# First loads, 5x5 weight chores and the exchange of the fourth image's input statistics: a rearranged start of a two-convolution kernel

## The chip, the cores and the metric

The kernel runs on one core of one Trainium2 chip. The metric is the device time of one execution in microseconds (us), lower is better.

## What is computed

Sixteen images of 32 channels and 128x128 pixels go through two residual blocks, each a group normalization and a convolution:

```python
def _gn(v, G=16, eps=1e-05):            # 16 groups of 2 channels, per image
    ...
    return ((g - m) / jnp.sqrt(s + eps)).reshape(v.shape)
...
x = x + _L0_conv_ref(_gn(x), L0_conv_weight, L0_conv_threshold)   # 3x3, weights masked by a threshold
x = x + _L1_conv_ref(_gn(x), L1_conv_kernel, L1_conv_bias)        # 5x5, plus bias
```

The mask of the 3x3 weights depends on the sums of their absolute values over the output channels and on the scalar threshold, so no 3x3 weight can be used before all the weights and the threshold are on the chip.

## The kernel before

**Halves and steps.** Each image is cut into an upper and a lower half, so there are 32 halves (`HALVES`). A half lies on 128 partitions as 4 bands of rows by 32 channels. TensorE works in steps: step s does the 3x3 convolution of half s and the 5x5 convolution of half s - 3 (`LAG` is 3). Steps 0 to 2 do the 3x3 alone (the lead), steps 3 to 31 do both, steps 32 to 34 the 5x5 alone. Every value and weight is split into a high and a low float16 (`hi`, `lo`), and three of the four products are taken. Within a step TensorE does the 3x3 pairs (144 matmuls, `pairs3_high`, `pairs3_low`), then the high 5x5 pairs (320 matmuls, `pairs5_high`), the 3x3 singles, the 5x5 singles (their end signals `a5_whole`) and the low 5x5 pairs (their end signals `b5_whole`). The loop body is the same code in all steps; step 3 is its first pass. I call the start of `pairs5_high` in a step its 5x5 start.

**Statistics.** A half is normalized with the statistics of its whole image. VectorE takes them with `stats_in` (of `x_bands`, 4 instructions of 0.66 us for a half) and `stats_out` (of `mid`, the first block's result). The statistics of a group lie on several partitions and are combined in one of two ways. For images 0 and 1's input and image 0's middle, TensorE mixes them (`set_apart`, `mix_members`, `combine`). For all others they are exchanged through DRAM: VectorE's `aggregate` signals `mv_ready`, ScalarE's queue writes `mv` to `mv_scratch` (`spread_stats`), waits until that has landed, and reads all of it back to every partition as `every_mv` (`gather_stats`); then VectorE's `group_stats`, ScalarE's root and VectorE's `scale_of` give mean and scale. In what follows x2 and x3 are the input statistics of the third and fourth image (halves 4, 5 and 6, 7), mid1 the middle statistics of the second. Before, x2, mid1 and x3 are three exchanges, told off after steps 2, 3 and 4; from then on one exchange every two steps carries a middle and an input image together.

**Orders.** Each engine runs its own list in the order in which it is written, and waits for semaphores in that order. On ScalarE, at step s: take the 5x5 result of half s - 4 out of PSUM (`take_conv5`, 4 instructions), give TensorE leave for the 5x5 start (`x5_hi_go`), gather the exchange of step s - 1, normalize and split the coming halves, and last `spread_stats(s)`, which waits for `mv_ready`. GpSimd adds the 5x5 result to `mid` (`add_out`, L369), and in the lead it issues the 16 transfers of half 1 (L363). SyncE's queue (SPq) carries nearly all transfers: `load_bands` (L261, 4 of 288 KB for a half), `load_own` (L250), `move_mid` (L269, 16 transfers inside the chip), `store_out` (L255). The weights of both convolutions, threshold, mixing matrix and bias are loaded once: the 3x3 weights, the threshold and the matrix by ScalarE's queue (ACTq), the 5x5 weights and the bias by SPq behind three halves' bands.

**Last steps.** From half `LATE` on, ScalarE takes out two of the four banks of a 5x5 result and VectorE the other two (`take_late`, L757); before it, ScalarE takes all four.

## Time and profile before

| what | value |
|---|---|
| median of 3 runs | 823.47 us (822.88 to 823.75) |
| profiled execution, its own time | 823.28 us |
| its span in the trace | 821.5 us |
| TensorE matmul busy | 756.0 us (92%) |
| VectorE busy | 608.8 us (74%) |
| ScalarE busy | 333.9 us (41%) |
| GpSimd busy | 265.3 us (32%) |
| mean granted TensorE clock | 0.98 |

The span is what the trace covers; 1.8 us of the execution lie around it. Busy shares are means over the whole span, while the steps at the start and at the end have other limits than those between.

### The profile page before, as it was taken

Reading aid. Unit: us, or ns where it says so; the run is one execution under the profiler, and the core shown is the slowest. Engines: PE = TensorE matmul, PEld = TensorE weight load, DVE = VectorE, ACT = ScalarE, POOL = GpSimd, SP = SyncE. Lnnn points to the kernel's source line nnn. Section 1 sums busy time; section 2 is a strip of 40 time slices with the busy share of each in tenths; the row PEclk is TensorE's granted clock in tenths of the full one; section 3 lists DMA queues with packets and bytes.
Section 4 is the critical chain, followed back from the end, with each engine's and each line's share of the span. In section 5 each row is a group of like instructions: output and inputs, shape, how many; then the busy total and the mean of one; then the engine's idle time right before and its main releaser. Section 6 shows DMA issues by size and latency. Waiting matters only on the chain.

```text
span 821.5 us, 67804 instructions
## 1 busy us (share of the span) xinstructions
PE 756.0 (92%) x32292; PEld 528.7 (64%) x32292; DVE 608.8 (74%) x970; ACT 333.9 (41%) x289; POOL 265.3 (32%) x161
## 2 busy tenths in 40 slices
PE   0585898899999999999999999999999999998996
PEld 0252484568767667767766766776776676676664
DVE  2888757797878969787879878787878786663341
ACT  0252314344443636344443536353443436362420
POOL 1021034044434332233434343222434343322360
PEclk9997898999999999999999999999999999999998
DMA  9879399989997989899897979898997956673424
GB/s 203 158 143 224 75 217 227 230 205 220 195 222 171 220 195 221 196 218 212 202 217 168 219 183 227 196 225 198 215 219 181 220 116 161 137 167 86 99 51 102
DMA packets 234400, 150.76 MB, mean 184 GB/s; under 512 B 18752, under 2 KB 227712, under 8 KB 230272
## 3 DMA queue, kind: packets, MB, share of 16 engines
q1 hardware_dynamic: 227200, 143.93, 80.8%
q10 hardware_dynamic: 6464, 5.24, 2.7%
q0 software_dynamic: 704, 1.25, 0.6%
q8 instruction: 10, 0.16, 0.1%
q14 instruction: 22, 0.18, 0.1%
HBM read 75.86 MB, written 33.59 MB: 133 GB/s over the span
## 4 chain that ended last, share of the span: by engine, by line
PE 82%; DVE 8%; DMA 4%; issue 2%; DVEq 1%; ACT 1%; ACTq 1%
PE psum L868 63%; PE psum L886 20%; DMA every_mv<-mv_scratch 2%; DVE bn_in L615 2%; DMA thr<-L_conv_threshold_dram 1%; DVE x_lo L719 1%; DVE bn_out L747 1%; DMA mv_scratch<-mv 1%; DVE mid L739 1%; DVEq L742 1%; ACT conv_out L468 0%; ACTq L506 0%; ACTq L486 0%; DVE x_bands L691 0%; ACT x_hi L399 0%
## 5 line engine op out<-in xcount | busy, mean ns | idle before, releaser
L369 POOL TENSOR_TENSOR mid<-mid,conv_out 128x512 f32<-128x512 f32 x120 | 246.0, 2082 | 484.0 <-ACT conv_out L468 484.0
L868 PE MATMUL psum<-x_hi,s_hi 32*64 32x512 f16 x6656 | 201.3, 384 | 18.2 <-ACTq L506 6.2
L868 PE MATMUL psum<-x_lo,s_hi 32*64 32x512 f16 x6656 | 200.1, 383 | 5.9 <-DVE x_lo L719 5.9
L868 PE MATMUL psum<-x_hi,s_lo 32*64 32x512 f16 x6656 | 199.7, 381 | 0.0
L868 PEld LDWEIGHTS psum<-x_hi,s_hi 32*64 32x64 f16 x6656 | 122.0, 105 | 85.9 <-issue 11.2
L868 PEld LDWEIGHTS psum<-x_hi,s_lo 32*64 32x64 f16 x6656 | 133.6, 105 | 53.6 <-issue 4.3
L868 PEld LDWEIGHTS psum<-x_lo,s_hi 32*64 32x64 f16 x6656 | 108.9, 104 | 83.8 <-issue 11.6
L739 DVE SCALAR_TENSOR_TENSOR mid<-psum,unscale,x_own 128x1024 f32<-128x1024 f32 x64 | 79.1, 1278 | 90.5 <-PE psum L886 90.4
L468 ACT ACTIVATE conv_out<-psum,bias,unscale 128x512 f32<-128x512 f32 x120 | 83.7, 777 | 69.7 <-PE psum L868 60.7
L392 ACT ACTIVATE x_hi<-x_bands 128x2304 f16<-128x2304 f32 x31 | 65.6, 2117 | 106.2 <-PE psum L886 106.2
L727 DVE TENSOR_TENSOR x_lo<-mid_bands,x_hi 128x2560 f16<-128x2560 f32 x32 | 93.8, 2932 | 6.9 <-PE psum L868 6.8
L431 ACT ACTIVATE x_hi<-mid_bands 128x2560 f16<-128x2560 f32 x31 | 72.5, 2339 | 50.8 <-PE psum L886 48.8
L385 ACT ACTIVATE root<-gvar 128x1 f32<-128x1 f32 x32 | 6.5, 203 | 207.7 <-DVE gvar L668 175.2
L438 ACT ACTIVATE mid_bands<-mid_bands,nbias,gscale 128x2560 f32<-128x2560 f32 x31 | 78.2, 2524 | 16.0 <-DVE nbias L682 13.6
L747 DVE BATCH_NORM_STATS2 bn_out<-mid 128x6 f32<-128x512 f32 x128 | 79.1, 680 | 4.1
L719 DVE TENSOR_TENSOR x_lo<-x_bands,x_hi 128x2304 f16<-128x2304 f32 x32 | 80.7, 2522 | 0.6 <-ACT x_hi L392 0.2
L615 DVE BATCH_NORM_STATS2 bn_in<-x_bands 128x6 f32<-128x512 f32 x128 | 76.7, 663 | 2.6 <-DMA x_bands<-x_dram 2.6
L886 PE MATMUL psum<-x_hi,s_hi 32*32 32x512 f16 x4096 | 74.3, 378 | 1.8 <-issue 1.7
L886 PE MATMUL psum<-x_hi,s_lo 32*32 32x512 f16 x4096 | 73.4, 376 | 0.0
L691 DVE TENSOR_SCALAR x_bands<-x_bands,gmean,gscale 128x2304 f32<-128x2304 f32 x29 | 67.8, 2339 | 0.5 <-ACT x_hi L403 0.4
L886 PE MATMUL psum<-x_lo,s_hi 32*32 32x512 f16 x4096 | 66.2, 377 | 1.4 <-issue 1.4
L886 PEld LDWEIGHTS psum<-x_hi,s_hi 32*32 32x32 f16 x4096 | 53.6, 88 | 19.7 <-issue 15.7
(91 smaller groups left out, 338.3 us busy)
## 6 DMA issues: line engine op xcount, KB each, us to landing
x_own<-x_dram SPq DMA_DIRECT2D x128, 256.0 KB, 5.0
mid_bands<-mid SPq DMA_DIRECT2D x372, 80.0 KB, 3.4
out_dram<-mid SPq DMA_DIRECT2D x116, 256.0 KB, 5.3
x_bands<-x_dram SPq DMA_DIRECT2D x96, 288.0 KB, 6.1
x_bands<-x_dram SPq DMA_DIRECT2D x32, 272.0 KB, 6.9
mid_bands<-mid SPq DMA_DIRECT2D x124, 64.0 KB, 2.9
every_mv<-mv_scratch ACTq DMA_DIRECT2D x17, 256.0 KB, 4.1
out_dram<-mid SPq DMA_DIRECT2D x20, 128.0 KB, 2.4
```

The lines of the kernel that those rows point to most:

```text
L369: nc.gpsimd.tensor_tensor(m, m, conv_out[:, b, :], ALU.add).then_inc(out_added, 1)
L431: nc.scalar.activation(x5_hi[:, :, 2:2 + W], mid_bands[:, k % MB_SLOTS, :, :], ACT.Copy).then_inc(hi5_done, 1)
L438: nc.scalar.activation(v, v, ACT.Identity, bias=nbias[:, at], scale=gscale[:, at]).then_inc(act_scaled, 1)
L468: nc.scalar.activation(conv_out[:, b, :], psum[:, X5_BANK + b, :], ACT.Identity, bias=bias[:, 0:1], scale=unscale[:, 1:2]).then_inc(conv5_ ...
L615: nc.vector.bn_stats(bn_in[:, h // 2 % 2, h % 2, b, :], rows.rearrange("p a w -> p (a w)")).then_inc(bn_x, 1)
L691: nc.vector.tensor_scalar(v, v, gmean[:, 0:1], gscale[:, 0:1], ALU.subtract, ALU.mult).then_inc(scaled, 1)
L719: nc.vector.tensor_tensor(x3_lo[:, :, 2:2 + W], x_bands[:, h % XB_SLOTS, :, :], x3_hi[:, :, 2:2 + W], ALU.subtract).then_inc(x3_lo_go, 1)
L727: nc.vector.tensor_tensor(x5_lo[:, :, 2:2 + W], mid_bands[:, k % MB_SLOTS, :, :], x5_hi[:, :, 2:2 + W], ALU.subtract).then_inc(x5_lo_go, 1)
L739: nc.vector.scalar_tensor_tensor(mid[:, h % MID_SLOTS, at, :], psum[:, X3_BANK + at.start:X3_BANK + at.stop, :], unscale[:, 0:1], x_own[:, ...
L747: nc.vector.bn_stats(bn_out[:, h % 2, b, :], mid[:, h % MID_SLOTS, b, :]).then_inc(bn_mid, 1)
L868: ins = nc.tensor.matmul(psum[2 * C * J:2 * C * (J + 1), bank + i, :].rearrange("p (a w) -> p a w", a=A), w[quad(i), at:at + 2, :].rearran ...
L886: ins = nc.tensor.matmul(psum[quad(j), bank + i, :].rearrange("p (a w) -> p a w", a=A), w[quad(i), at, :], src[quad(i), j + dy:j + dy + A ...
```

## The change

The change does six things. (1) Two of the four copies of the 3x3 weights are issued by SPq ahead of all bands, the other two by ACTq ahead of the threshold. (2) The 5x5 weights move ahead of the third half's bands, and the bias moves to ACTq with a semaphore of its own. (3) The largest absolute 5x5 weight is looked for while TensorE mixes image 0's statistics; the 5x5 weights are scaled by GpSimd, rounded to float16 by ScalarE after its `high3(3)`, and the low part is made by GpSimd. (4) Bands of halves 6 and 7 are issued right behind `move_mid(2)`, no longer behind the wait for `a5_whole`. (5) x3 and mid1 share one exchange after step 3, so there is none after step 4. (6) `LATE` is one half earlier.

```diff
-        mv_dram = nc.dram_tensor("mv_scratch", (N + 1, P, 2, 2), F32, kind="Internal").ap()
+        mv_dram = nc.dram_tensor("mv_scratch", (N, P, 2, 2), F32, kind="Internal").ap()
...
         def exchanged(s):
 
-            if s in (2, LAG + 1):
-                return [("x", 2 if s == 2 else LAG)]
+            if s == 2:
+                return [("x", 2)]
             if not (LAG <= s < HALVES and s % 2):
                 return []
-            return [("mid", s // 2)] + ([("x", (s + 3) // 2)] if LAG < s and (s + 3) // 2 < N else [])
+            return [("mid", s // 2)] + ([("x", (s + 3) // 2)] if (s + 3) // 2 < N else [])
...
-        LATE = HALVES - LAG
+        LATE = HALVES - LAG - 1
...
+            for q in range(Q // 2):
+                sp.dma_start(w3[quad(q), :, :], w3_dram.rearrange("i a b o -> i (a b) o")).then_inc(w3_loaded, 16)
             load_bands(0)
             load_bands(1)
-            load_bands(2)
             for q in range(Q):
                 sp.dma_start(w5[quad(q), :, :], w5_dram.rearrange("i a b o -> i (a b) o")).then_inc(w_loaded, 16)
-                sp.dma_start(bias[quad(q), :], bias_dram.rearrange("(o a) -> o a", a=1)).then_inc(w_loaded, 16)
+            load_bands(2)
...
             load_bands(5)
             move_mid(2)
+            load_bands(6)
+            load_bands(7)
             sp.wait_ge(a5_whole, 1)
             load_own(LAG + 1)
             move_edges(1, 1, 0)
-            load_bands(6)
-            load_bands(7)
...
+            pool.wait_ge(w5_bounded, 1)
+            nc.gpsimd.tensor_scalar(w5[:, :, :], w5[:, :, :], wfac[:, 1:2], None, ALU.mult).then_inc(w5_scaled, 1)
+            pool.wait_ge(w5_hi_made, 1)
+            nc.gpsimd.tensor_tensor(s5_lo[:, :, :], w5[:, :, :], s5_hi[:, :, :], ALU.subtract).then_inc(w5_split, 1)
...
             def high_w5():
 
-                act.wait_ge(w5_bounded, 1)
-                nc.scalar.activation(s5_hi[:, :, :], w5[:, :, :], ACT.Identity,
-                                     bias=zeros[:, 0:1], scale=wfac[:, 1:2]).then_inc(w5_hi_made, 1)
+                act.wait_ge(w5_scaled, 1)
+                nc.scalar.activation(s5_hi[:, :, :], w5[:, :, :], ACT.Copy).then_inc(w5_hi_made, 1)
...
-            for q in range(Q):
+            for q in range(Q // 2, Q):
                 act.dma_start(w3[quad(q), :, :], w3_dram.rearrange("i a b o -> i (a b) o")).then_inc(w3_loaded, 16)
             act.dma_start(thr[:, :], thr_dram.rearrange("(a o) -> a o", a=1).to_broadcast([P, 1])).then_inc(w3_loaded, 16)
             act.dma_start(mix_in[:, :], mix_dram).then_inc(mix_loaded, 16)
+            for q in range(Q):
+                act.dma_start(bias[quad(q), :], bias_dram.rearrange("(o a) -> o a", a=1)).then_inc(bias_loaded, 16)
...
-                    high_w5()
                 elif s == 2:
                     high3(3)
+                    high_w5()
                     take_root(("mid", 0))
...
             set_apart("x", 0)
+            dve.wait_ge(w_loaded, 16 * Q)
+            largest(w5, 1)
             dve.drain().then_inc(bank3_go, 1)
...
-            dve.wait_ge(w_loaded, 16 * 2 * Q)
-            largest(w5, 1)
             power_of_two(1)
...
-            dve.wait_ge(w5_hi_made, 1)
-            nc.vector.scalar_tensor_tensor(s5_lo[:, :, :], w5[:, :, :], wfac[:, 1:2], s5_hi[:, :, :],
-                                           ALU.mult, ALU.subtract).then_inc(w5_split, 1)
             normalize5_first()
...
             stats_out(LAG)
-            aggregate("mid", LAG // 2, mv_ready)
             low3(LAG + 1)
+            stats_in(2 * LAG, range(BANKS))
+            stats_in(2 * LAG + 1, range(BANKS))
+            aggregate("mid", LAG // 2)
+            aggregate("x", LAG, mv_ready)
...
-                if s == LAG + 1:
-                    for h in (2 * LAG, 2 * LAG + 1):
-                        stats_in(h, range(BANKS))
-                    aggregate("x", LAG, mv_ready)
-                elif exchanged(s):
+                if exchanged(s):
```

How the instructions move on three engines follows, with the line numbers of each version. First SyncE's queue at the first pass of the loop, before: the first rows are the end of `load_bands(5)` and `move_mid(2)`.

```order
L261 DMA x_bands<-x_dram 32x2304 x3
L261 DMA x_bands<-x_dram 32x2176
L269 DMA mid_bands<-mid 32x5x128 x2
L269 DMA mid_bands<-mid 32x4x128 x2
L269 DMA mid_bands<-mid 32x5x128 x8
L269 DMA mid_bands<-mid 32x4x128 x2
L269 DMA mid_bands<-mid 32x5x128 x2
L250 DMA x_own<-x_dram 32x16x128 x4
L280 DMA mid_bands<-mid 32x128 x2
L261 DMA x_bands<-x_dram 32x2176
L261 DMA x_bands<-x_dram 32x2304 x6
L261 DMA x_bands<-x_dram 32x2176
```

The same place of SyncE's queue with the change:

```order
L263 DMA x_bands<-x_dram 32x2304 x3
L263 DMA x_bands<-x_dram 32x2176
L271 DMA mid_bands<-mid 32x5x128 x2
L271 DMA mid_bands<-mid 32x4x128 x2
L271 DMA mid_bands<-mid 32x5x128 x8
L271 DMA mid_bands<-mid 32x4x128 x2
L271 DMA mid_bands<-mid 32x5x128 x2
L263 DMA x_bands<-x_dram 32x2176
L263 DMA x_bands<-x_dram 32x2304 x6
L263 DMA x_bands<-x_dram 32x2176
L252 DMA x_own<-x_dram 32x16x128 x4
```

The eight transfers of bands 6 and 7 (2.3 MB) now stand ahead of the `x_own` loads, which keep the wait for `a5_whole`.

Second, VectorE from the normalization of half 4 on, at the end of step 3, before:

```order
L691 TENSOR_SCALAR x_bands<-x_bands,gmean,gscale 128x2304
L696 MEMSET x_bands 32x128
L739 SCALAR_TENSOR_TENSOR mid<-psum,unscale,x_own 128x1024 x2
L747 BN_STATS bn_out<-mid 128x6 x4
L625 BN_AGGR mv<-bn_out 128x2
L719 TENSOR_TENSOR x_lo<-x_bands,x_hi 128x18x128
L727 TENSOR_TENSOR x_lo<-mid_bands,x_hi 128x20x128
```

With the change:

```order
L702 TENSOR_SCALAR x_bands<-x_bands,gmean,gscale 128x2304
L707 MEMSET x_bands 32x128
L750 SCALAR_TENSOR_TENSOR mid<-psum,unscale,x_own 128x1024 x2
L758 BN_STATS bn_out<-mid 128x6 x4
L730 TENSOR_TENSOR x_lo<-x_bands,x_hi 128x18x128
L626 BN_STATS bn_in<-x_bands 128x6 x8
L636 BN_AGGR mv<-bn_out 128x2
L636 BN_AGGR mv<-bn_in 128x2
L738 TENSOR_TENSOR x_lo<-mid_bands,x_hi 128x20x128
```

The signal for the exchange, which stood at the first BN_AGGR, now stands at the last one, behind the low part of half 4 and the eight statistics instructions of halves 6 and 7.

Third, ScalarE at the same place, from the write and read of the x2 exchange on. Before:

```order
L475 DMA mv_scratch<-mv 128x4
L481 DMA every_mv<-mv_scratch 128x512
L385 ACTIVATE root<-gvar 128x1
L438 ACTIVATE mid_bands<-mid_bands,nbias,gscale 128x2560
L460 ACTIVATE mid_bands<-zeros 32x256
L392 ACTIVATE x_hi<-x_bands 128x18x128
L431 ACTIVATE x_hi<-mid_bands 128x20x128
L475 DMA mv_scratch<-mv 128x4
L468 ACTIVATE conv_out<-psum,bias,unscale 128x512 x4
L481 DMA every_mv<-mv_scratch 128x512
L385 ACTIVATE root<-gvar 128x1
```

With the change:

```order
L484 DMA mv_scratch<-mv 128x4
L490 DMA every_mv<-mv_scratch 128x512
L393 ACTIVATE root<-gvar 128x1
L445 ACTIVATE mid_bands<-mid_bands,nbias,gscale 128x2560
L467 ACTIVATE mid_bands<-zeros 32x256
L400 ACTIVATE x_hi<-x_bands 128x18x128
L438 ACTIVATE x_hi<-mid_bands 128x20x128
L484 DMA mv_scratch<-mv 128x4
L477 ACTIVATE conv_out<-psum,bias,unscale 128x512 x4
L490 DMA every_mv<-mv_scratch 128x512
L393 ACTIVATE root<-gvar 128x1 x2
```

The rows are in the same order, with a second root behind the last read. The second `mv_scratch` write, behind which `take_conv5(0)` and TensorE's leave for step 4's 5x5 start stand, now waits for the later signal of VectorE.

## Rows read from the trace of the kernel before

**Rows 1.** Busy by stretch: us, PE, PEld, DVE, ACT, POOL, PEclk, DMA share, GB/s.

```profile
109.42:137.43 28.01, 24.37 (x1021) 17.99 (x1012) 19.68 (x33) 10.36 (x9) 9.00 (x6) 0.93 1.14 228
...
137.43:167.22 29.79, 26.22 (x1016) 15.64 (x1008) 19.43 (x34) 10.29 (x9) 7.26 (x5) 0.89 1.03 208
...
167.22:190.02 22.80, 22.80 (x1020) 16.93 (x1012) 21.99 (x39) 11.24 (x11) 10.05 (x4) 1.00 0.98 218
```

**Rows 2.** Chain of waits in order of time (start us, us, what), first load.

```profile
3.83 11.01 DMA thr<-L_conv_threshold_dram
```

**Rows 3.** DMA issues (KB, us to landing), made at 2.1, 2.1 and 5.0.

```profile
w<-L_conv_weight_dram ACTq DMA_DIRECT2D x1, 36.0 KB, 7.8
...
x_bands<-x_dram SPq DMA_DIRECT2D x1, 288.0 KB, 8.2
...
x_bands<-x_dram SPq DMA_DIRECT2D x1, 288.0 KB, 9.5
```

**Rows 4.** Timeline (start us, us, engine, operation), VectorE before step 3.

```profile
28.85 0.17 DVE L643 COPY members<-psum 128x16 f32<-128x16 f32 x1 [0.77 <-PE psum L930]
...
57.67 0.98 DVE L569 TENSOR_REDUCE bound<-w 128x1 f32<-128x800 f32 x1
```

**Rows 5.** Timeline, page part 5 and timeline again: GpSimd.

```profile
55.71 9.21 POOL L363 DMA_DIRECT2D mid_bands<-mid  x16 [50.73 <-DVE mid L739]
...
L369 POOL TENSOR_TENSOR mid<-mid,conv_out 128x512 f32<-128x512 f32 x120 | 246.0, 2082 | 484.0 <-ACT conv_out L468 484.0
...
782.64 6.41 POOL L377 TENSOR_SCALAR mid<-mid,bias 128x2048 f32<-128x2048 f32 x1
```

**Rows 6.** Timeline: ScalarE root of image 0, SyncE move_mid(2).

```profile
67.46 0.20 ACT L385 ACTIVATE root<-gvar 128x1 f32<-128x1 f32 x1 [3.95 <-DVE gvar L653]
...
72.10 11.58 SPq L269 DMA_DIRECT2D mid_bands<-mid  x16
```

**Rows 7.** Timeline: third image's input statistics and their exchange.

```profile
82.14 2.48 DVE L615 BATCH_NORM_STATS2 bn_in<-x_bands 128x6 f32<-128x512 f32 x4 [2.62 <-DMA x_bands<-x_dram]
...
85.05 0.34 ACTq L475 DMA_DIRECT2D mv_scratch<-mv  x1
...
88.31 0.33 ACTq L481 DMA_DIRECT2D every_mv<-mv_scratch  x1
...
91.74 0.41 DVE L660 SCALAR_TENSOR_TENSOR product<-every_mv,mix_in 128x128 f32<-128x128 f32 x1 [4.39 <-DMA every_mv<-mv_scratch]
```

**Rows 8.** Chain of waits: later exchange transfers.

```profile
108.76 10.11 DMA every_mv<-mv_scratch
...
132.43 7.69 DMA mv_scratch<-mv
...
140.14 8.00 DMA every_mv<-mv_scratch
```

**Rows 9.** Timeline of TensorE in its first whole step.

```profile
81.56 3.20 PE L868 MATMUL psum<-x_hi,s_hi 32*64 32x512 f16 x51 [5.24 <-issue]
...
97.96 0.39 PE L886 MATMUL psum<-x_hi,s_hi 32*32 32x512 f16 x4 [1.74 <-issue]
```

**Rows 10.** Busy time by stretch, columns as in rows 1.

```profile
88.00:92.00 4.00, 3.93 (x207) 2.47 (x192) 0.26 (x1) 0.00 (x0) 0.00 (x0) 1.00 0.24 74
```

**Rows 11.** Timeline: VectorE and ScalarE, steps 4 and 5.

```profile
101.79 2.50 DVE L719 TENSOR_TENSOR x_lo<-x_bands,x_hi 128x2304 f16<-128x2304 f32 x1
...
127.16 4.83 DVE L615 BATCH_NORM_STATS2 bn_in<-x_bands 128x6 f32<-128x512 f32 x8
...
132.86 2.79 ACT L468 ACTIVATE conv_out<-psum,bias,unscale 128x512 f32<-128x512 f32 x4 [3.02 <-DVE mv L625]
...
122.27 2.52 ACT L438 ACTIVATE mid_bands<-mid_bands,nbias,gscale 128x2560 f32<-128x2560 f32 x1 [1.19 <-DVE nbias L682]
```

**Rows 12.** Timeline of TensorE at the last 5x5 starts.

```profile
759.61 4.61 PE L868 MATMUL psum<-x_hi,s_hi 32*64 32x512 f16 x160 [2.96 <-ACTq L506]
...
778.25 4.61 PE L868 MATMUL psum<-x_hi,s_hi 32*64 32x512 f16 x160 [1.61 <-ACTq L506]
```

More of the change, by code:

```diff
@@ L125, in two_blocks @@
         w5_bounded = sem("w5_bounded")
+        bias_loaded = sem("bias_loaded")
+        w5_scaled = sem("w5_scaled")
         w5_hi_made = sem("w5_hi_made")
@@ L373, in _ @@
                     add_out(k, b)
-                if k == LATE:
+                if k == LATE + 1:
+                    pool.wait_ge(bias_loaded, 16 * Q)
                     pool.wait_ge(norm2, HALVES)
@@ L463, in take_conv5 @@
             def take_conv5(k, b):
+                if k == 0 and b == 0:
+                    act.wait_ge(bias_loaded, 16 * Q)
                 act.wait_ge(b5_whole, k + 1)
@@ L500, in _ @@
                         take_conv5(k, b)
-                if HALVES < s <= LAST + LAG:
-                    act.wait_ge(late_out, s - HALVES)
+                if LATE + LAG < s <= LAST + LAG:
+                    act.wait_ge(late_out, s - LATE - LAG)
                 if s == LAG:
@@ L752, in take_late @@
                 if k == LATE:
+                    dve.wait_ge(bias_loaded, 16 * Q)
                     dve.wait_ge(out_added, BANKS * LATE)
@@ L810, in _ @@
             stats_out(LAG)
-            aggregate("mid", LAG // 2, mv_ready)
             low3(LAG + 1)
+            stats_in(2 * LAG, range(BANKS))
+            stats_in(2 * LAG + 1, range(BANKS))
+            aggregate("mid", LAG // 2)
+            aggregate("x", LAG, mv_ready)
             for s in range(LAG + 1, STEPS):
                 gathered = exchanged(s - 1)
-                if s > HALVES:
+                if s > LATE + LAG:
                     take_late(s - 1 - LAG)
                 low5(s - LAG)
-                if s > HALVES:
+                if s > LATE + LAG:
                     add_late(s - 1 - LAG)
-                just_now = ("x", (s + 1) // 2) in gathered
-                if has3(s + 1) and not just_now:
+                if has3(s + 1):
                     normalize3(s + 1)
@@ L829, in _ @@
                     scale_of(stat)
-                if just_now:
-                    normalize3(s + 1)
                 if s % 2:
```

## The prediction

> **What bounds the kernel now.** I read the chain of waits first. From step 6 to the tail it is TensorE's matmuls alone. I then cut the span at TensorE's 5x5 starts and read busy time by stretch. In the third row of [rows 1] one whole step takes 22.80 us, all of it busy, at full clock; the chain shows this step repeated until the tail, so nothing in the change can shorten it. The two steps before it take 28.01 and 29.79 us, 12.2 us more than two full ones, with idle time and a granted clock of 0.93 and 0.89. Ahead of them lie 109.4 us of start. So there are three places where time can come from: the start, these two steps, and the stops of 2.96 and 1.61 us in the tail [rows 12].
>
> What fills the start is told by the chain: first the threshold, which lands 11.01 us after its issue, at 14.8 us [rows 2], then VectorE nearly without a gap until step 3, then the x2 exchange. What fills the two steps are the mid1 and x3 exchanges: 10.11 us for one read, 7.69 and 8.00 us for the next write and read [rows 8], while the x2 exchange took only 3.3 us and 3.4 us [rows 7]. The difference is the traffic beside it: at 88 to 92 us the DMA share is 0.24, in the two steps it is 1.14 and 1.03 [rows 1, 10].
>
> **Weights first by two queues.** The last 3x3 weights, issued at 2.1 us, land at 9.9 us, the fourth band issued at the same time at 10.3, the eighth band at 5.0 + 9.5 = 14.5 us [rows 3], the threshold at 14.8 [rows 2]. Counted in partition rows, ACTq had then moved 4 x 32 of weights and 128 of threshold, SPq 8 x 32 of bands: 256 each, and 128 each at 9.9 and 10.3. The queues take turns row by row, whatever a row holds. With the change 64 + 128 = 192 ACTq rows bring the threshold; SPq's first 192 rows are 64 of weights and 128 of bands, which is the content that had landed at 10.3 us. The bands are issued 0.9 us later, so between 10.3 and 11.2; I take 10.8, **4.0 us earlier**. Bounds: 2.2 us if only its earlier issue counted (two issues fewer ahead), 4.5 at best.
> In the Trainium skill, "DMA: Bandwidth & Descriptors", section "Issuing engines are not separate DMA queues", using several issuing engines only saves issue time. By that rule this term would be 2.2 us. It is a rival below.
>
> **The 5x5 chores.** VectorE's search for the largest weight (0.98 us) moves into a wait of 0.77 us [rows 4]: it adds 0.3 us there and takes 1.0 us away before step 3. The 5x5 weights have landed by then: they are 0.4 MB behind two halves, whose last band came at 14.5, and VectorE gets there at about 24. So VectorE runs 3.7 us ahead of before until 54, then 4.7. On the other side GpSimd is free only when its 16 transfers are issued, 55.71 + 9.21 - 3.7 = 61.2 us. Its scaling costs 6.41 x 800/2048 = 2.5 us, its subtraction 2.08 x 800/512 = 3.3 us [rows 5]. ScalarE rounds from 63.8 to 64.9 and only then takes image 0's root, at 64.9 where before it was 67.46 [rows 6]: of the 4.7 us only 2.6 remain. The low weights are ready at 68.2, before ScalarE has the first 5x5 input (69.2). This delay is covered: x2's statistics wait 2.62 us for half 5's band [rows 7], and that band depends on SPq alone, which moves by 3.7. If GpSimd is slower by more than some 1.5 us, each further one counts.
>
> **The x2 exchange in traffic.** It starts 3.7 us earlier, at 85.05 - 3.7 = 81.3. But `move_mid(2)`, issued from 72.10 for 11.58 us [rows 6], ends at 80.0 now, and behind it come bands 6 and 7 at once, no longer after the first pass. Those are 2.3 MB, at about 218 GB/s, between the 208 and 228 of [rows 1], 10.6 us: DMA is full until about 93. By turns of rows the 128 small rows of the write take as long as in [rows 8], 7.7; I take 7.4, until 88.7. The read (128 rows) is in traffic for 4 of its us and then free: 7.0, between the free 3.4 and the full 10.1. x2 lands at **95.7**, where a free exchange would have landed at 88.0.
>
> **The joint exchange.** From x2's landing to the end of the low part of half 4 VectorE needed 101.79 + 2.50 - 91.74 = 12.55 us [rows 7, 11]. Now come the eight statistics, 4.83 us, and one more aggregate, 0.3: `mv_ready` at 95.7 + 17.7 = 113.4 instead of 101.9. What is queued behind it on ScalarE is `take_conv5(0)` and the leave for the 5x5 start. That engine already shows this wait, 3.02 us before 132.86 [rows 11]. Add 0.4 and 2.8 for four takings: TensorE's 5x5 start of step 4 comes at **116.7, 7.3 us later** than 109.42. TensorE itself would be there at 109.42 - 2.6 plus the slower code loads below, 2 to 6: at 109 to 113.
> After that x3 is known, and the 12.2 us of the two steps fall away, except for a lower clock after the stop of step 4. In the two steps busy time was 1.6 and 3.4 us over a full step's 22.80 [rows 1]; I take 2.1, since the step after the stop has no second one. Is the joint read in time for step 5? It is issued at 116.9 and takes 8.0. Behind the read that landed at 108.76 + 10.11 = 118.9, ScalarE began to normalize at 122.27 [rows 8, 11], 3.4 us for one statistic; for two I take 6.8, so 131.7. Then it normalizes for 2.5 us and splits half 5 in about as long: ready at 136.7. The 144 pair matmuls of a 3x3 take 144 x 4.61/160 = 4.1 us [rows 12], so step 5 starts at 116.7 + 22.8 - 4.1 + 2.1 = 137.5. In time by 0.8 us.
> Sum of this part: +7.3 - 12.2 + 2.1 = **-2.8 us**. The weights' 4.0 us are already in it, since they set the 81.3.
>
> **The tail.** Step 32's stop of 2.96 us becomes one of 1.61, since ScalarE takes two banks and VectorE, idle there, the others [rows 12]: **-1.35 us**. The bias, now on ACTq, is needed a hundred us later: nothing.
>
> **Sum.** 823.28 (the profiled execution's own time) - 2.8 - 1.35 = 819.1. The runs' median is 0.2 higher, so I give **819.2 us**. A measurement here tells 0.2% (1.6 us) from no change.
>
> **Code loading.** TensorE stands still for 5.24 us at 76.3 to 81.56 and for 1.74 us before 97.96 with nothing to wait for but its own code [rows 9], which this pass meets for the first time; the long stop lies in full DMA traffic, the short one in none. Bands 6 and 7 now bring traffic to two or three more such loads. I expect 2 to 6 us more, hidden in the wait for 116.7.
> The skill's "Runtime: NRT & Kernel Launch", section "Instruction fetch mechanics", calls such crossings mostly hidden. The 5.24 us disagree; by the rule the pass would end earlier and the sum would be the same.
>
> **The rivals.**
> *Bands 6 and 7 don't hurt x2* (its write and read keep 3.3 and 3.4 us): `mv_ready` at 88.0 + 17.7 = 105.7, 5x5 start at 109.0, no stop behind it: -0.4 - 12.2 - 1.35, so 809.3. For it: the traffic is of known length, and the write's rows are tiny. Against: [rows 8]. Chance 0.15.
> *The queues' rule* holds: everything in the start is 1.8 us later, 821.0. Chance 0.08.
> *Code loading takes over*: three further stops at 5.2 instead of 1.4 to 1.7 are +11 us on the first pass, and the 5x5 start comes at 109.42 - 2.6 + 11 = 117.8 plus a clock not yet recovered, some 1.6: +2.7, 821.8. Chance 0.17.
> *Slower*: exchanges in traffic take their worst row. x2's read takes 10.1: 5x5 start at 119.8, +3.1. The joint read takes 10.1 too, half 5 is ready at 120 + 10.1 + 6.8 + 5.0 = 141.9, 1.3 after the step's start at 140.6, and the stop lowers the clock once more, 2.1: 823.3 - 4.15 + 3.1 + 1.3 + 2.1 = 825.6. It decides once both exchanges together are more than 4 us over my figures. For it: 10.11 us is a row of this trace; against: the joint read meets no backlog of bands. Chance 0.15.
> *The forecast*, 816 to 822: chance 0.45.
>
> **Numbers.** Range 810 to 825: it reaches to the first rival and leaves out most of the last and half of the first. Faster by over 0.2%: nearly all of the forecast, the first rival, the rule and part of code loading, 0.70. Within 0.2%: 0.15. Slower: 0.15.
>
> **What would show it.** In the trace after: first mask instruction of VectorE near 10.9 us; image 0's root near 65; x2's write at 81 and its read back near 96; DMA full from 82 to 93; `mv_ready` near 113; a stop of TensorE before step 4's 5x5 start near 116.7, none before step 6; one stop of 1.6 us where 2.96 was. Wrong would make it: an x2 landing outside 93 to 99, a first pass ending after 112, or a second stop before step 5.

## The result: 814.4 us, 1.1% faster than before

| | changed | before, beside it |
|---|---|---|
| median | 814.38 us | 823.61 us |
| runs | 4 (813.69 to 816.45) | 4 (822.88 to 825.56) |
| ratio | 0.9887 (0.9871 to 0.9902) | |
| profiled execution, its span | 814.51 us, 812.7 us | 823.28 us, 821.5 us |
| mean granted clock | 0.985 | 0.98 |

The kernel became 9.2 us faster; 4.3 us were forecast. The time lies inside the range and has the sign of the forecast, but the gain is twice as large, so one of the steps must be wrong. (Two later timings of the same change, further down, give gains of 7.3 and 8.1 us.) Each step is now compared, in the order of the program. In the changed kernel most line numbers are higher than before, by 2 to 11: L873 and L891 are the matmuls, L484 and L490 the exchange's write and read, L517 the leave for the 5x5 start.

**The start.** DMA issues of the changed kernel (KB, us from issue to landing), made at 2.1 and 1.66 us:

```profile
x_bands<-x_dram SPq DMA_DIRECT2D x1, 288.0 KB, 5.1
...
thr<-L_conv_threshold_dram ACTq DMA_DIRECT2D x1, 0.5 KB, 6.2
```

Timeline of VectorE in the changed kernel (start us, us, engine, operation, idle before and who ended it):

```profile
7.96 0.46 DVE L603 TENSOR_REDUCE score<-w 128x9 f32<-128x288 f32 x1 [6.15 <-DMA thr<-L_conv_threshold_dram]
...
21.01 0.98 DVE L580 TENSOR_REDUCE bound<-w 128x1 f32<-128x800 f32 x1
22.13 0.17 DVE L654 COPY members<-psum 128x16 f32<-128x16 f32 x1
```

The threshold lands at 7.86 us; [rows 2] had 14.84. So the first mask instruction starts at 7.96, not near 10.9, and the copy of the mixed sums at 22.13 where [rows 4] has 28.85: 6.7 us earlier. The search for the largest weight (21.01) fills the wait before that copy, as expected. Between the two VectorE takes the eight statistics of the first two halves without waiting for their bands. In other executions it does wait for the second half's bands, as shown below, so these are the next floor of the start.

**The 5x5 chores.** Timelines of GpSimd, ScalarE and VectorE in the changed kernel:

```profile
58.37 2.29 POOL L368 TENSOR_SCALAR w<-w,wfac 128x800 f32<-128x800 f32 x1
61.64 1.71 POOL L370 TENSOR_TENSOR s_lo<-w,s_hi 128x800 f16<-128x800 f32 x1 [0.98 <-ACT s_hi L431]
...
60.69 0.87 ACT L431 ACTIVATE s_hi<-w 128x800 f16<-128x800 f32 x1 [4.20 <-POOL w L368]
61.47 0.19 ACT L393 ACTIVATE root<-gvar 128x1 f32<-128x1 f32 x1
...
75.07 2.47 DVE L626 BATCH_NORM_STATS2 bn_in<-x_bands 128x6 f32<-128x512 f32 x4 [0.48 <-DMA x_bands<-x_dram]
```

ScalarE's rounding waits for GpSimd and image 0's root follows at 61.47, 6.0 us earlier than in [rows 6]. GpSimd's subtraction takes 1.71 us, not 3.3. Half 5's statistics still wait for their band, now 0.48 us instead of the 2.62 of [rows 7]: the chores are covered, though only just.

**The x2 exchange.** Timeline of SyncE's queue, ScalarE's queue and VectorE, then busy time by stretch (us, PE, PEld, DVE, ACT, POOL, PEclk, DMA share, GB/s), changed kernel:

```profile
76.78 5.14 SPq L263 DMA_DIRECT2D x_bands<-x_dram  x8
77.98 0.35 ACTq L484 DMA_DIRECT2D mv_scratch<-mv  x1
85.77 0.35 ACTq L490 DMA_DIRECT2D every_mv<-mv_scratch  x1
91.90 0.39 DVE L671 SCALAR_TENSOR_TENSOR product<-every_mv,mix_in 128x128 f32<-128x128 f32 x1 [11.62 <-DMA every_mv<-mv_scratch]
...
84.00:88.00 4.00, 0.74 (x44) 0.30 (x24) 0.00 (x0) 0.00 (x0) 0.00 (x0) 1.00 1.04 230
88.00:92.00 4.00, 1.71 (x73) 1.27 (x80) 0.10 (x1) 0.00 (x0) 0.00 (x0) 0.64 0.48 114
```

Bands 6 and 7 are issued at 76.78, the write behind them takes 7.8 us until 85.77 and the read 6.1 us until 91.90. Before it was 3.3 and 3.4 [rows 7]. Although the exchange starts 7.1 us earlier than before, x2 lands 0.2 us later. The DMA share beside it is 1.04 from 84 to 88 us and 0.48 from 88 to 92, when the bands are in; before, with the exchange in about the same place, [rows 10] had 0.24.

**From x2 to step 6.** Timelines of ScalarE's queue, ScalarE, TensorE and VectorE at step 4's 5x5 start, then the stretches between 5x5 starts, changed kernel:

```profile
109.65 0.33 ACTq L484 DMA_DIRECT2D mv_scratch<-mv  x1
110.08 2.78 ACT L477 ACTIVATE conv_out<-psum,bias,unscale 128x512 f32<-128x512 f32 x4 [8.09 <-DVE mv L636]
112.95 6.26 PE L873 MATMUL psum<-x_hi,s_hi 32*64 32x512 f16 x160 [3.46 <-ACTq L517]
112.97 0.33 ACTq L490 DMA_DIRECT2D every_mv<-mv_scratch  x1
117.11 1.31 DVE L671 SCALAR_TENSOR_TENSOR product<-every_mv,mix_in 128x128 f32<-128x128 f32 x1 [2.23 <-DMA every_mv<-mv_scratch]
...
112.95:116.00 3.05, 3.05 (x64) 1.56 (x72) 1.84 (x2) 0.00 (x0) 3.05 (x3) 0.51 0.79 172
...
112.95:137.44 24.49, 24.49 (x1009) 15.96 (x1016) 18.95 (x38) 11.23 (x11) 8.10 (x5) 0.93 1.07 229
137.44:160.20 22.76, 22.76 (x1016) 17.31 (x1008) 17.70 (x21) 9.44 (x8) 8.02 (x5) 1.00 0.93 205
```

ScalarE's taking of the 5x5 result waits 8.09 us for the joint `mv_ready`, and TensorE stops for 3.46 us before its 5x5 start at 112.95, 3.5 us later than the 109.42 of [rows 1]. The 160 matmuls behind the stop take 6.26 us instead of 4.6, since the granted clock is 0.51, about the lower level of 1.2 GHz, up to 116. The joint read is issued 3.3 us after the write, but the write is not what it waits for: it lands 1.8 us after its issue, and the read stands behind ScalarE's four takings. The read takes 4.1 us. After that there is no stop: 24.5 and 22.8 us stand where [rows 1] has 28.01 and 29.79. Step 6's 5x5 start is at 160.20, before it was at 167.22: **7.0 us** are won by here.

**Code loading.** Timeline of TensorE in the first pass, changed kernel:

```profile
76.18 1.73 PE L873 MATMUL psum<-x_hi,s_hi 32*64 32x512 f16 x51 [2.31 <-issue]
81.30 2.61 PE L873 MATMUL psum<-x_hi,s_lo 32*64 32x512 f16 x83 [1.41 <-issue]
90.29 0.61 PE L891 MATMUL psum<-x_hi,s_hi 32*32 32x512 f16 x4 [5.55 <-issue]
```

Three stops with no releaser, and two more of 1.09 and 1.01 us follow at 98 and 102: 11.4 us in sum. Before it was 8.4: the 5.24 and 1.74 of [rows 9] and one of 1.44 us between them, which [rows 9] leaves out. That these are code loads is seen in the DMA queues. Between 84.7 and 90.3 us the changed kernel has

```profile
q8 instruction: 1, 0.02, 1.5%
```

that is, one transfer of 16 KB on the instruction queue, and one such transfer lies in each of these stops or ends within 0.4 us ahead of it, in both kernels; from step 4's 5x5 start to step 6's this queue moves nothing. The pass ends before 109.5 all the same, ahead of the leave at 112.95.

**The tail.** Timeline of TensorE at the 5x5 starts of steps 32 and 33, changed kernel:

```profile
750.79 4.60 PE L873 MATMUL psum<-x_hi,s_hi 32*64 32x512 f16 x160 [1.61 <-ACTq L517]
769.43 4.60 PE L873 MATMUL psum<-x_hi,s_hi 32*64 32x512 f16 x160 [1.62 <-ACTq L517]
```

The stop of 2.96 us of [rows 12] is one of 1.61. From step 6's 5x5 start to the end it is 652.5 us, before 654.3: **1.8 us** are won here, 1.35 of them by this stop.

### The profile page after: what moved, and what is told of

Same layout as the page of the kernel before. It is cut to its first block, busy times and chain, and to the rows that moved or that the text cites. A ratio compares the mean times of both kernels' runs of the same rounds, so it can differ in the third digit from the quotient of the medians.

```text
span 812.7 us, 67805 instructions
## 1 busy us (share of the span) xinstructions
PE 751.7 (92%) x32292; PEld 503.0 (62%) x32292; DVE 615.3 (76%) x971; ACT 332.3 (41%) x287; POOL 264.6 (33%) x161
## 4 chain that ended last, share of the span: by engine, by line
PE 85%; DMA 5%; SPq 4%; DVE 3%; issue 1%; DVEq 0%; ACT 0%; ACTq 0%
PE psum L873 65%; PE psum L891 20%; DMA x_bands<-x_dram 3%; SPq L271 1%; DVE bn_in L626 1%; SPq L263 1%; SPq L252 1%; DMA mv_scratch<-mv 1%; DMA every_mv<-mv_scratch 1%; DVE x_lo L730 1%; ACT conv_out L477 0%; DVE x_bands L702 0%; SPq L278 0%; DVE mid L750 0%; DVEq L753 0%
## 5 line engine op out<-in xcount | busy, mean ns | idle before, releaser
L376 POOL TENSOR_TENSOR mid<-mid,conv_out 128x512 f32<-128x512 f32 x118 | 241.2, 2075 | 481.5 <-ACT conv_out L477 481.5
L873 PE MATMUL psum<-x_hi,s_hi 32*64 32x512 f16 x6656 | 199.6, 383 | 16.4 <-ACTq L517 8.3
L873 PE MATMUL psum<-x_lo,s_hi 32*64 32x512 f16 x6656 | 197.5, 380 | 6.3 <-DVE x_lo L730 5.3
L873 PE MATMUL psum<-x_hi,s_lo 32*64 32x512 f16 x6656 | 196.5, 377 | 1.4 <-issue 1.4
L873 PEld LDWEIGHTS psum<-x_hi,s_hi 32*64 32x64 f16 x6656 | 107.3, 105 | 98.5 <-ACTq L517 10.2
L873 PEld LDWEIGHTS psum<-x_hi,s_lo 32*64 32x64 f16 x6656 | 127.0, 104 | 58.9 <-issue 2.8
L873 PEld LDWEIGHTS psum<-x_lo,s_hi 32*64 32x64 f16 x6656 | 102.6, 104 | 87.2 <-issue 9.8
L891 PE MATMUL psum<-x_hi,s_hi 32*32 32x512 f16 x4096 | 74.7, 380 | 6.6 <-issue 6.6
L891 PE MATMUL psum<-x_hi,s_lo 32*32 32x512 f16 x4096 | 74.3, 380 | 0.0
L891 PEld LDWEIGHTS psum<-x_hi,s_hi 32*32 32x32 f16 x4096 | 54.3, 88 | 24.5 <-issue 20.6
L891 PE MATMUL psum<-x_lo,s_hi 32*32 32x512 f16 x4096 | 68.0, 384 | 0.1
```

The source lines that it names most:

```text
L376: nc.gpsimd.tensor_tensor(m, m, conv_out[:, b, :], ALU.add).then_inc(out_added, 1)
L873: ins = nc.tensor.matmul(psum[2 * C * J:2 * C * (J + 1), bank + i, :].rearrange("p (a w) -> p a w", a=A), w[quad(i), at:at + 2, :].rearran ...
L891: ins = nc.tensor.matmul(psum[quad(j), bank + i, :].rearrange("p (a w) -> p a w", a=A), w[quad(i), at, :], src[quad(i), j + dy:j + dy + A ...
```

## The experiments

"Its before" is the kernel before, timed on the same chip together with it. All kernels compute the whole reference. The theories: **T1**, the small transfers ahead give more than turns of rows allow, and this is most of the gain; **T2**, bands 6 and 7 beside the x2 exchange take back what the joint exchange gives; **T3**, the one half more for `take_late` gives 1.35 us.

| kernel | median us (its before) | ratio (interval) |
|---|---|---|
| weights part alone | 818.68 (825.24) | 0.9925 (0.9897 to 0.9952) |
| changed, weights part undone | 822.64 (825.24) | 0.9970 (0.9954 to 0.9985) |
| changed, weights behind the first half | 817.85 (825.24) | 0.9915 (0.9886 to 0.9944) |
| changed, exchanges apart, bands 6, 7 late | 816.39 (825.24) | 0.9898 (0.9867 to 0.9929) |
| changed, second time | 816.18 (823.50) | 0.9918 (0.9888 to 0.9947) |
| changed, bands 6, 7 behind x2 | 809.05 (823.50) | 0.9823 (0.9790 to 0.9856) |
| the same, chores as before | 807.57 (823.50) | 0.9799 (0.9765 to 0.9832) |
| changed, all weights by SPq | 816.06 (823.50) | 0.9899 (0.9867 to 0.9932) |
| changed, third time | 815.46 (823.57) | 0.9897 (0.9846 to 0.9947) |
| changed, `LATE` undone | 820.19 (823.57) | 0.9948 (0.9926 to 0.9970) |
| changed, chores undone | 816.49 (823.57) | 0.9898 (0.9848 to 0.9948) |
| bands 6, 7 behind x2, chores as before, bands 4, 5 early | 808.13 (823.57) | 0.9810 (0.9760 to 0.9860) |
| changed, `LATE` undone, second time | 819.45 (823.07) | 0.9954 (0.9938 to 0.9970) |
| before, second profile | 822.45 (823.07) | one run |
| bands 6, 7 behind x2, chores as before, all weights by SPq | 806.45 (823.07) | 0.9806 (0.9788 to 0.9823) |

**The weights part alone, and everything but it.** The first is the kernel before with this edit; the second is the changed kernel with it undone.

```diff
+            for q in range(Q // 2):
+                sp.dma_start(w3[quad(q), :, :], ...).then_inc(w3_loaded, 16)
             load_bands(0)
...
-            for q in range(Q):
+            for q in range(Q // 2, Q):
                 act.dma_start(w3[quad(q), :, :], ...).then_inc(w3_loaded, 16)
```

> The kernel before with one part of the change: two quarters of the 3x3 weights issued by SyncE's queue ahead of all bands, two by ScalarE's ahead of the threshold. Theory (the start alone gave most of the gain, about 7.0 us, and the tail 1.8; the joint exchange with early bands is worth about nothing): VectorE's first mask instruction near 8 us, x2's write near 78, x2 landed near 85, total about 7 us below before, 816.6 (815.8 to 817.8). Rival (the forecast's sum: the start gives less than 4 us by itself and the rest of the change the other 5): 819.5 to 820.5.

> The changed kernel with the weights' part undone: all four quarters by ScalarE's queue behind one another, bands first on SyncE's. Theory: VectorE's first mask instruction back near 14.9 us, everything up to step 6 some 6.5 to 7 us later than in the changed kernel, total 821.0 (820.3 to 821.8). Rival (the joint exchange and the early bands carry the gain): 816 to 818.

The weights part alone wins 6.6 us (by its interval 4.0 to 8.5), everything else together 2.6 (1.2 to 3.8); the sum is the 9.2 measured. Both times lie above the ranges expected, since the kernel before took 825.24 us on this chip; the distances to it are the expected ones. T1 holds for the size of the weights part by these times. The one profile of that kernel doesn't show it: it is of its slowest execution (821.79 us), in which the mask starts at 10.57 us, only 4.4 us earlier than before. In the first kernel the two later stops stay, as its timeline of TensorE shows:

```profile
131.92 2.79 PE L870 MATMUL psum<-x_lo,s_hi 32*64 32x512 f16 x48 [4.57 <-DVE x_lo L721]
...
161.65 0.65 PE L870 MATMUL psum<-x_lo,s_hi 32*64 32x512 f16 x16 [2.74 <-DVE x_lo L721]
```

In the second, VectorE starts the mask late, and x2's write and read (ScalarE's queue, then VectorE's first use) show that the exchange suffers without the weights part too:

```profile
14.53 0.45 DVE L601 TENSOR_REDUCE score<-w 128x9 f32<-128x288 f32 x1 [12.73 <-DMA thr<-L_conv_threshold_dram]
...
84.73 0.35 ACTq L482 DMA_DIRECT2D mv_scratch<-mv  x1
89.05 0.35 ACTq L488 DMA_DIRECT2D every_mv<-mv_scratch  x1
99.61 0.38 DVE L669 SCALAR_TENSOR_TENSOR product<-every_mv,mix_in 128x128 f32<-128x128 f32 x1 [12.58 <-DMA every_mv<-mv_scratch]
```

4.3 and 10.6 us: a sum of 14.9, against 13.9 in the changed kernel and 6.7 before.

**Where the weights stand.** Two edits of the changed kernel: SPq issues its two weight quarters behind `load_bands(0)`; or SPq issues all four ahead of the bands, and ACTq begins with the threshold.

```diff
-            for q in range(Q // 2): sp.dma_start(w3...)
             load_bands(0)
+            for q in range(Q // 2): sp.dma_start(w3...)
```
```diff
-            for q in range(Q // 2): sp.dma_start(w3...)
+            for q in range(Q): sp.dma_start(w3...)
...
-            for q in range(Q // 2, Q): act.dma_start(w3...)
```

> The changed kernel with SyncE's two weight quarters issued behind the four transfers of the first half's bands instead of ahead of them; ScalarE's queue is as changed. If the queues take turns row by row from the start, the last of weights and threshold lands at about 10.8 us, 3 us later than in the changed kernel, total 817.3. If what matters is only what stands ahead of the threshold on ScalarE's own queue, it lands near 8 and SyncE's quarters near 10, total 816.5. If the ahead-of-all-bands place matters because weights and threshold then move before the bands' backlog forms, threshold and weights land later than 11 us: 818 or more.

> The changed kernel with all four quarters of the 3x3 weights on SyncE's queue ahead of the bands and the threshold alone first on ScalarE's. If a place ahead of the bands' backlog is what counts, weights and threshold have all landed by 5 us, VectorE starts near 5 and then waits for the second half's band (which lands near 16 to 18): total 0 to 2 us below the changed kernel. If ScalarE's queue is slow whatever stands on it, no difference.

DMA issue of the threshold at 1.66 us and timeline of VectorE in the first kernel:

```profile
thr<-L_conv_threshold_dram ACTq DMA_DIRECT2D x1, 0.5 KB, 6.4
...
10.67 0.45 DVE L603 TENSOR_REDUCE score<-w 128x9 f32<-128x288 f32 x1 [8.87 <-DMA w<-L_conv_weight_dram]
```

Timeline of VectorE in the second:

```profile
5.60 0.45 DVE L601 TENSOR_REDUCE score<-w 128x9 f32<-128x288 f32 x1 [3.79 <-DMA w<-L_conv_weight_dram]
...
18.71 2.47 DVE L624 BATCH_NORM_STATS2 bn_in<-x_bands 128x6 f32<-128x512 f32 x4 [2.64 <-DMA x_bands<-x_dram]
23.01 0.17 DVE L652 COPY members<-psum 128x16 f32<-128x16 f32 x1
```

In the first kernel the bands start at 0.73 us as they did before, and still the threshold lands at 8.1. What VectorE waits for are SPq's two quarters, issued at 3.5 us and later. This run decides on the turns. By turns the threshold, at the end of ACTq's 192 rows, would be due with SPq's first 192 rows, the first half's four bands and the two quarters, near the 10.8 us of the expectation. These rows did come at 10.6. The threshold came at 8.1, when SPq had landed three bands, some 100 rows; the fourth landed at 9.5. That the mask starts near 10.8 here is therefore no support for the turns. The time of this kernel, 0.9915 of its before, can't be told from that of the changed kernel (0.9887, 0.9918 and 0.9897 in three timings): that the two quarters stand ahead of the bands, and not behind the first half's, is not shown to gain anything.

With all of the weights ahead the mask starts at 5.60, but VectorE then waits for bands, 2.64 us before the second half's statistics, and the copy comes at 23.01, no earlier than 22.13. The time stays that of the changed kernel.

**The changed kernel twice more**, to see how much of this varies.

> The changed kernel once more, on the chip of the next three, so that they can be read against it: 9 us below before, as measured first.

> The changed kernel once more on the chip of the next three, to read them against it: 7 to 9 us below before.

The change wins 7.3 and 8.1 us here, where the first timing gave 9.2. The mask starts at 7.64 and 6.91 us, the copy comes at 22.94 and 21.48. Over all eleven profiles with the weights ahead by two queues the mask starts between 5.75 and 10.57 us (in seven of them up to 8.3, in four from 9.9 on) and the copy comes between 21.5 and 24.7; with the old order the three profiles give 14.94 (behind the threshold of [rows 2]), 14.80 and 14.53. Where the mask starts before 8 us, the copy comes between 21.5 and 23.2 without following it, since VectorE then mostly waits for the second half's bands. The x2 write varies too. VectorE and ScalarE's queue in the second profile:

```profile
18.64 2.47 DVE L626 BATCH_NORM_STATS2 bn_in<-x_bands 128x6 f32<-128x512 f32 x4 [1.03 <-DMA x_bands<-x_dram]
...
78.99 0.35 ACTq L484 DMA_DIRECT2D mv_scratch<-mv  x1
90.09 0.35 ACTq L490 DMA_DIRECT2D every_mv<-mv_scratch  x1
```

**Exchanges apart.** The changed kernel with x3 and mid1 exchanged apart and bands 6 and 7 loaded behind the first pass, as before.

```diff
-            if s == 2:
-                return [("x", 2)]
+            if s in (2, LAG + 1):
+                return [("x", 2 if s == 2 else LAG)]
...
-            load_bands(6)
-            load_bands(7)
             sp.wait_ge(a5_whole, 1)
             load_own(LAG + 1)
             move_edges(1, 1, 0)
+            load_bands(6)
+            load_bands(7)
```

> The changed kernel with separate exchanges for mid1 and x3 and bands 6 and 7 behind the wait for a5_whole, as before; weights, chores and LATE as changed. Theory (joint exchange with early bands nets to zero: 5x5 start of step 4 ten us earlier, two slow steps of 12 us instead of one stop): 814.5 (813.5 to 815.7). Rival (the joint exchange was worth the forecast's 2.8 us or more): 817 to 819.

0.9898 against 0.9887, 0.9918 and 0.9897 of the changed kernel, on other chips: parts 4 and 5 of the change together show no gain. One or two microseconds either way could hide in the intervals. Without them x2's write and read take 3.0 and 4.0 us, and the stops of 3.43, 2.86 and 1.43 us in steps 5 and 6 are back.

**Bands 6 and 7 held until x2 has landed.** The changed kernel with one wait more.

```diff
             move_mid(2)
+            sp.wait_ge(mv_in, 16)
             load_bands(6)
             load_bands(7)
```

> The changed kernel, but SyncE issues bands 6 and 7 only when x2's read has landed (a wait on mv_in), so that exchange has the DMA to itself. Theory (the early bands take back what the joint exchange gives, by slowing x2's write and read): x2's write and read take 3.3 and 3.4 us again, x2 lands near 85 instead of 92, the 5x5 start of step 4 comes 1 to 6 us earlier (TensorE's code loads then meet the bands' traffic), total 2 to 4 us below the changed kernel. Rival (TensorE's first pass bounds that place, not x2): same as the changed kernel within 1 us.

Timeline of ScalarE's queue, VectorE, SyncE's queue, ScalarE and TensorE, and the stretch of the exchange:

```profile
78.48 0.35 ACTq L485 DMA_DIRECT2D mv_scratch<-mv  x1
81.62 0.35 ACTq L491 DMA_DIRECT2D every_mv<-mv_scratch  x1
85.06 0.48 DVE L672 SCALAR_TENSOR_TENSOR product<-every_mv,mix_in 128x128 f32<-128x128 f32 x1 [4.29 <-DMA every_mv<-mv_scratch]
85.05 4.78 SPq L263 DMA_DIRECT2D x_bands<-x_dram  x8
...
103.75 2.79 ACT L478 ACTIVATE conv_out<-psum,bias,unscale 128x512 f32<-128x512 f32 x4 [3.52 <-PE psum L874]
107.38 4.57 PE L874 MATMUL psum<-x_hi,s_hi 32*64 32x512 f16 x160
...
78.00:82.00 4.00, 4.00 (x128) 2.15 (x118) 2.74 (x6) 0.00 (x0) 0.00 (x0) 0.75 0.29 44
```

This is the cleanest of the tests: 7.1 us faster than the changed kernel on the same chip. Write and read are at 3.1 and 3.4 us, DMA at 0.29; `mv_ready` comes at 103.0, ScalarE takes the 5x5 result when TensorE has it, and TensorE reaches the 5x5 start at 107.38 without a stop; in the changed kernel's second profile, on the same chip, it was 114.56, 7.2 us later. T2 holds, and its price is larger than the 2 to 4 us I had expected of it. Beside the kernel with the exchanges apart (0.9898 of its before, here 0.9823, and the intervals don't meet) it shows too what the joint exchange is worth once x2's is left alone: some 6 us.

**The chores.** ScalarE rounds with the scale, in its old place (`high_w5` in step 1), and VectorE makes the low part as before; first in the kernel with the added wait, then in the changed kernel.

```diff
-            nc.gpsimd.tensor_scalar(w5[:, :, :], w5[:, :, :], wfac[:, 1:2], None, ALU.mult).then_inc(w5_scaled, 1)
...
-            nc.gpsimd.tensor_tensor(s5_lo[:, :, :], w5[:, :, :], s5_hi[:, :, :], ALU.subtract).then_inc(w5_split, 1)
...
+            nc.vector.scalar_tensor_tensor(s5_lo[:, :, :], w5[:, :, :], wfac[:, 1:2], s5_hi[:, :, :],
+                                           ALU.mult, ALU.subtract).then_inc(w5_split, 1)
```

> As the run with bands 6 and 7 behind x2's read, and in addition the 5x5 weights are scaled by ScalarE and split by VectorE as before (the search for the largest stays in its new place). If GpSimd's share of the chores delays TensorE's first whole step (x_lo of half 3 came 3.7 us late in the changed kernel) and that step now bounds, total a further 1 to 3 us lower. If not, no difference.

> The changed kernel with the 5x5 weights scaled by ScalarE and split by VectorE as before. In the changed kernel the delay by GpSimd is covered by the wait for half 5's band and later by x2's landing, so the root of image 0 comes 2 us earlier and x_lo of step 3 three us earlier, and the total stays (within 1 us of the changed kernel). If the delay were not covered, 2 to 3 us below it.

No difference outside the intervals: 807.57 beside 809.05, and 816.49 beside 815.46. VectorE arrives earlier at half 5's statistics and waits 3.53 and 3.67 us there for the band, instead of 0.5 to 1.0.

**Bands 4 and 5 early.** To the kernel with the added wait and the chores as before: is that band the next bound?

```diff
             load_own(1)
+            load_bands(4)
+            load_bands(5)
             sp.wait_ge(mid_made, PIECES)
...
-            load_bands(4)
...
-            load_bands(5)
```

> The version with bands 6 and 7 behind x2's read and the chores back, and in addition bands 4 and 5 issued in the first load, where DMA stood idle from 36 to 40 us, instead of behind the moves of half 0. VectorE's wait of 3.5 us for half 5's band goes, x2's write starts 3 us earlier; TensorE's code loads of the first pass meet less traffic. If x2 still bounds step 4's start: 2 to 3 us below that version (807.6), 804.5 to 805.5. If TensorE's first pass bounds it by now: 0 to 1.5 us below.

Timeline of ScalarE in this kernel:

```profile
68.71 2.52 ACT L418 ACTIVATE x_hi<-mid_bands,nbias,gscale 128x2560 f16<-128x2560 f32 x1 [8.45 <-DMA mid_bands<-mid]
```

The wait for the band is gone, but the copies inside the chip now land behind these bands: ScalarE waits 8.45 us for `mid_bands`, TensorE 6.28 us for ScalarE's leave at 71.77, and x2's write starts no earlier (81.95). One wait took the place of the other, and neither expected outcome came: 808.13 us beside 807.57 is no gain.

**`LATE` undone**, in the changed kernel, twice, and the kernel before once more.

```diff
-        LATE = HALVES - LAG - 1
+        LATE = HALVES - LAG
...
-                if k == LATE + 1:
+                if k == LATE:
```

> The changed kernel with LATE where it was. The stop before the 5x5 start of step 32 is 2.96 us again instead of 1.61; total 1.35 us above the changed kernel (0.8 to 2.2). Rival (the sharing by VectorE costs elsewhere what it saves): no difference.

> The changed kernel with LATE where it was, again, since it came out 4.7 us above the changed kernel where 1.35 was expected. If the excess is the start's variation (first mask instruction at 10.5 us in that profile) plus the stop of step 32 and the clock lost behind it, the profile shows the stop of 2.96 us each time, the next 5x5 start 18.6 or 20.3 us later, and a ratio to before of 0.990 to 0.996. If it was chance, the ratio is 0.991 or below.

> The kernel before, profiled a second time. If the landing of the threshold varies from execution to execution as it does with the weights first (VectorE's first mask instruction stood between 6.3 and 10.6 us in ten profiles), it should stand somewhere between 12 and 18 us here instead of 14.94; if it is fixed by what stands ahead in the queues, at 14.9 within 0.5. The last 5x5 starts after step 32's stop come 18.6 us apart if no clock is lost there, 20.3 if it is.

It costs 4.7 us on the same chip, where T3 says 1.35. Timeline of TensorE at the last 5x5 starts and the stretch behind the stop, the second of the two, then the kernel before profiled again:

```profile
753.33 7.48 PE L873 MATMUL psum<-x_hi,s_hi 32*64 32x512 f16 x160 [2.94 <-ACTq L517]
774.83 4.61 PE L873 MATMUL psum<-x_hi,s_hi 32*64 32x512 f16 x160 [1.60 <-ACTq L517]
...
753.33:756.00 2.67, 2.67 (x56) 1.26 (x64) 0.02 (x1) 0.00 (x0) 2.67 (x3) 0.50 0.68 186
756.00:759.00 3.00, 3.00 (x72) 1.35 (x64) 1.97 (x5) 0.00 (x0) 2.14 (x2) 0.50 0.66 146
```
```profile
758.78 4.60 PE L868 MATMUL psum<-x_hi,s_hi 32*64 32x512 f16 x160 [2.95 <-ACTq L506]
777.41 4.60 PE L868 MATMUL psum<-x_hi,s_hi 32*64 32x512 f16 x160 [1.61 <-ACTq L506]
...
758.78:762.00 3.22, 3.22 (x120) 1.90 (x128) 0.02 (x1) 0.00 (x0) 3.22 (x3) 1.00 0.71 193
```

The stops are equal, 2.94 and 2.95 us. But behind the first the granted clock is 0.50 (the 1.2 GHz level) for some 5.7 us, and the next 5x5 start comes 21.50 us later instead of 18.63, so 2.9 us are lost a second time. In the other profile with `LATE` undone it is 20.27 (1.6 lost), and so it is for the weights part alone (20.20), which has the old `LATE` too. Both profiles of the kernel before lose nothing.

**All together, and all weights by SPq**: the wait before bands 6 and 7, the chores as before, and the order of weights of the earlier test.

> The version with bands 6 and 7 behind x2's read and the chores back, with all 3x3 weights on SyncE's queue ahead of the bands and the threshold first on ScalarE's. VectorE starts near 5.6 us and is then held by the second half's bands, so image 0's mix is taken up at 23.0 us, 1.1 us before that version's profile (24.07): ratio to before 0.001 to 0.002 below its 0.980. If the start does not reach through to step 4 any more (TensorE's code loads bound it), no difference.

806.45 us (806.18 to 807.01), 16.6 us under its before. It has the lowest median of all, but the other kernels with the held bands lie within some 2.6 us of it and were timed on other chips, so only the wait is shown to matter. Its mask starts at 5.29 us, and from step 3 on TensorE's longest stops are two code loads, 5.05 and 6.12 us.

## Why the forecast was half of the gain

**The step that failed** is the one under "Weights first by two queues": "The queues take turns row by row, whatever a row holds." From it came a threshold that lets VectorE start at 10.8, 4.0 us earlier, "4.5 at best". It rested on two counts in the old order. The first is right: 128 rows each, at 9.9 and 10.3 us. The second was misread: the 9.5 us of [rows 3] belong to the seventh band, issued at 4.76 and landed at 14.28; the eighth lands at 16.1. So when the threshold landed ACTq had moved 256 rows and SPq some 234, not 256 each. In the changed kernel the counts part further: at 7.86 us ACTq had moved its 192 rows, SPq its 64 of weights and two bands (landed at 5.5 and 7.2, the next ones after 9), some 130 to 140. With the weights behind the first half the threshold lands at 8.1 where turns give 10.8, with 192 rows against some 100. The term was 4.0 us, of which 3.7 at VectorE; measured it is 7.0 at the threshold, 6.7 at the copy, and 6.6 us of the whole time. In four of the eleven profiles the threshold lands at 9.8 to 10.5 us, near the forecast, in the other seven at 5.7 to 8.2, so 10.8 was the late end of what happens and not its middle. What shares the DMA engines out instead, why two weight quarters less on ACTq bring the threshold 7 us forward, and what moves the mask's start between 5.75 and 10.57 us from one execution to the next, stays open.

The rule in the Trainium skill ("DMA: Bandwidth & Descriptors", "Issuing engines are not separate DMA queues"), by which several issuing engines only save issue time, disagrees more: the threshold is issued 2.2 us earlier and lands 7.0 earlier, and in the latest of the eleven profiles still 4.4 earlier. My rival by that rule is out.

**How the error is made up**, from the times at which the forecast and the profiled execution meet: x2's write starts 3.3 us earlier than forecast (77.98, not 81.3); write and read take 0.5 less (13.9, not 14.4); from x2's landing to step 4's 5x5 start it is 21.0, as forecast; the clock behind the stop costs 1.7, not 2.1; from step 6 on 0.45 more than the tail's 1.35 are won, over 590 us in which I looked for nothing. 3.3 + 0.5 + 0.4 + 0.45 = 4.65 of the 4.8 us between 819.2 and 814.4. The landing of x2 at 91.9 us is also one of the forecast's own signs of being wrong, which allowed 93 to 99; the other two, a first pass ending after 112 and a second stop before step 5, did not come.

**Right, with numbers**: the largest weight adds 0.26 us (0.3); GpSimd's scaling takes 2.29 (2.5); the chores are covered by half 5's band, and both tests with the chores undone confirm it; the exchange in the traffic of bands 6 and 7 takes 13.9 us (14.4); `mv_ready` is 17.7 us behind x2 (17.7); the stop of step 4 and the lower clock behind it appear, a second stop doesn't; the stop of 2.96 us is 1.61.

**Right by luck or wrong in size**: GpSimd's subtraction was 1.6 us too dear, since I scaled a float32 addition. The joint read was put at 8.0 us and took 4.1, beside a DMA share of 0.79; I had taken it from a read in a step with 1.03. Both had cover. Code loading came as forecast (11.4 us of stops where 8.4 were, so 3.0 more of the 2 to 6 expected), hidden behind the leave. The "Runtime: NRT & Kernel Launch" page of the Trainium skill, section "Instruction fetch mechanics", calls such crossings mostly hidden; here a stop of 5.55 us stands on TensorE, and only the wait behind it hides it from the end.

**The rivals.** "Bands 6 and 7 don't hurt x2" was priced at 809.3 with 0.15. It did not happen, but the kernel in which it is made true by a wait takes 809.05. That its price is met is in part luck: the start's 3.3 us would put it at 806, and I have not traced the 3 us between. "Code loading takes over" needed three further long stops; there is one long stop (5.55 us), as there was before (5.24). "Slower" needed exchanges 4 us over my figures; x2's write was 0.4 over, its read 0.9 under, the joint read 3.9 under.

**What `LATE` is worth** I had as 1.35 us. Shown is that in the changed kernel its undoing costs 4.7 us, and that 1.6 and 2.9 of them stand in the traces as a lower clock after the stop. Not shown is why the same stop does this in three profiles and not in the two of the kernel before. So part of the 2.6 us of everything but the weights may be this clock, and the sum of the change by parts (weights 6.6, `LATE` 1.4 to 4, chores 0, exchange and bands 0) is closed only within it.

## What to carry over

A few small transfers that gate the whole kernel are worth splitting over two queues (6.6 us here); that they must also stand ahead of the large ones on both was not shown. A rule for how queues share the engines, fitted to two rows of one order, is no price for another order: give such a term a range, from what its earlier issue alone brings to a landing with nothing ahead, and look at more than one profile. A latency-bound exchange through DRAM (3 us for a write, 3.4 for a read) doubles in the traffic of a bulk load beside it: hold the bulk load back by a wait on the exchange's landing if nothing needs it yet, and price an earlier issue by what it collides with. Before calling a joint exchange a gain, read who is queued behind its later signal.
